# Who makes the last fourteen low halves of the probabilities, and when the first batch's rows are sent

## The reference, cut to what matters

```python
q, k, v = (x @ W for W in (Wq, Wk, Wv))             # 2 x 1024 x 16 x 64
w = softmax(einsum('bihd,bkhd->bhik', q, k) / 8)
x = layernorm(x + einsum('bhij,bjhd->bihd', w, v).reshape(b, s, 1024) @ Wo + bo)
logits = ...                                         # 8 per token, from a small softmax over x @ wqkv.T
top, idx = top_k(logits, 2); scores = softmax(top)
he = silu(x @ w1[e, :352].T) * (x @ w1[e, 352:].T) @ w2[e].T   # e: each of the token's two experts
out = layernorm(x + sum of the two he, weighted by scores)
```

## Time and profile before

| | us |
|---|---|
| median of 3 runs (lowest to highest) | 865.77 (865.43 to 865.95) |
| the profiled execution, its own time | 863.55 |
| span of the profile | 861.8 |
| PE busy | 765.6 (89%) |
| ACT busy | 687.8 (80%) |
| POOL busy | 673.9 (78%) |
| DVE busy | 537.6 (62%) |
| L882, the low halves on POOL | 541.0, 256 of 2.13 |
| L783 and L784, the two exponentials on ACT | 286.3 and 284.9, 256 of each |
| L429, the sends of rows on POOL | 32 of 0.99 |

### The profile page before, as it was taken

The page is one execution under the profiler, slowest core; times in us unless marked ns, Lnnn a source line. Parts: engine busy times, 40 slices in busy tenths (PEclk is TensorE's granted clock), DMA queues, the critical chain, the costliest instruction groups (busy, mean ns, idle before and its releaser), DMA issues. The chain is left out here.

```text
span 861.8 us, 22282 instructions
## 1 busy us (share of the span) xinstructions
PE 765.6 (89%) x9183; PEld 525.2 (61%) x9183; DVE 537.6 (62%) x907; ACT 687.8 (80%) x854; POOL 673.9 (78%) x430
## 2 busy tenths in 40 slices
PE   2889999999999999999999999999988657839991
PEld 0346565666666666666666666666655446729990
DVE  6856667666666676666866667766653167515673
ACT  3899999998989898999999898989889755214452
POOL 5799888888888797888898789999999962554441
PEclk9999999999999999999999999999999987959996
DMA  5603064303031211213040404031200041121212
GB/s 174 150 2 75 5 139 82 78 2 78 8 72 27 53 39 41 54 27 75 5 108 5 112 2 111 14 99 39 48 11 17 11 117 44 36 71 51 79 40 86
DMA packets 43138, 49.30 MB, mean 57 GB/s; under 512 B 6785, under 2 KB 27655, under 8 KB 42912
## 3 DMA queue, kind: packets, MB, share of 16 engines
q1 hardware_dynamic: 39872, 43.31, 20.4%
q0 software_dynamic: 2496, 4.24, 1.5%
q10 hardware_dynamic: 672, 0.33, 0.2%
HBM read 14.28 MB, written 9.25 MB: 27 GB/s over the span
## 5 line engine op out<-in xcount | busy, mean ns | idle before, releaser
L882 POOL TENSOR_TENSOR pl<-p,ph 128x1024 f16<-128x1024 f32 x256 | 541.0, 2130 | 70.2 <-ACT ph L784 69.6
L944 DVE TENSOR_REDUCE mx<-mps 128x1 f32<-128x1024 f32 x249 | 303.8, 1220 | 133.7 <-PE mps L619 131.6
L783 ACT ACTIVATE p<-sps,escale 128x1024 f32<-128x1024 f32 x256 | 286.3, 1118 | 51.2 <-PE sps L599 45.6
L784 ACT ACTIVATE ph<-sps,escale 128x1024 f16<-128x1024 f32 x256 | 284.9, 1113 | 0.0
L694 PE MATMUL pair_bank<-v,ph 128*128 128x65 f16 x2048 | 214.7, 193 | 16.8 <-POOL pl L882 15.2
L694 PEld LDWEIGHTS pair_bank<-v,ph 128*128 128x128 f16 x2048 | 190.4, 96 | 55.7 <-POOL pl L882 25.2
L696 PE MATMUL pair_bank<-v,ph 128*128 128x64 f16 x2048 | 214.4, 195 | 0.0
L698 PE MATMUL pair_bank<-v,pl 128*128 128x65 f16 x2048 | 214.0, 192 | 0.0
L696 PEld LDWEIGHTS pair_bank<-v,ph 128*128 128x128 f16 x2048 | 190.0, 97 | 27.6
L598 PE MATMUL sps<-q_hh,k_hl 128*128 128x512 f16 x512 | 194.1, 379 | 1.8 <-ACT ph L784 1.5
L599 PE MATMUL sps<-q_lm,k_h 65*128 65x512 f16 x512 | 194.7, 380 | 0.0
(11 more groups left out here) (256 smaller groups left out, 966.8 us busy)
## 6 DMA issues: line engine op xcount, KB each, us to landing
q_hh<-hi SPq DMA_DIRECT2D x60, 128.0 KB, 2.3
q_lm<-lo SPq DMA_DIRECT2D x30, 128.0 KB, 2.4
k_h<-hi SPq DMA_DIRECT2D x30, 128.0 KB, 2.5
k_hl<-hi SPq DMA_DIRECT2D x29, 128.0 KB, 2.6
k_hl<-lo SPq DMA_DIRECT2D x29, 128.0 KB, 2.6
sorted<-pad SPq DMA_DIRECT2D x1, 2990.0 KB, 16.8
xb<-sorted SPq DMA_DIRECT2D x46, 65.0 KB, 1.8
v<-in_w1T SPq DMA_DIRECT2D x8, 352.0 KB, 3.5
```

The lines of the kernel that those rows point to most:

```text
L783: nc.scalar.activation(p32[:, n % 4, :], sps[:, n % 2, :], ACT.Exp, bias=EXP_BIAS, scale=escale[:, 0:1])
L784: nc.scalar.activation(ph[:, n % 4, :], sps[:, n % 2, :], ACT.Exp, bias=EXP_BIAS, scale=escale[:, 0:1]).then_inc(s_exp, 1)
L882: nc.gpsimd.tensor_tensor(pl[:, n % 4, :], p32[:, n % 4, :], ph[:, n % 4, :], ALU.subtract).then_inc(s_subp, 1)
L944: nc.vector.tensor_reduce(mx[:, i // TB, i % TB:i % TB + 1], src, AX.X, ALU.max).then_inc(s_mx, 1)
```

## The change

The low halves of steps 242 to 255 are made by DVE instead of GpSimd, with a semaphore of their own, `s_subv`, on which PE's `values` waits from step 242 on. DVE makes that of step n + 2 at the end of its slot n, behind whatever else the slot holds and ahead of its part of the routing. All sixteen sends of batch 0 now stand in the attention loop: four in pair 14 (steps 2, 6, 10, 14) where six stood, and twelve in steps 1 to 12 of pair 15, where GpSimd has no low halves any more beyond step 1. `passed` moves from step 9 of pair 15 to step 0, DVE's first part of `owner` from step 10 to step 3. The loop over the last four sends at the beginning of the second block goes.

```diff
-              ("vector", 13, 11, "where", 0), ("pool", 13, 15, "where", 1), ("pool", 15, 9, "passed", 0),
-              ("vector", 15, 10, "owner", 0), ("pool", 15, 14, "owner", 1))
-SEND_AT = {divmod(PCH * 14 + (8 * n) // 3, PCH): n for n in range(12)}
+              ("vector", 13, 11, "where", 0), ("pool", 13, 15, "where", 1), ("pool", 15, 0, "passed", 0),
+              ("vector", 15, 3, "owner", 0), ("pool", 15, 14, "owner", 1))
+SEND_AT = {(14, 2): 0, (14, 6): 1, (14, 10): 2, (14, 14): 3, **{(15, n - 3): n for n in range(4, 2 * TB)}}
+LAST_LOW = PCH * (PAIRS - 1) + 2
...
+        s_subv = sem("s_subv")
...
-                pe.wait_ge(s_subp, n + 1)
+                if n < LAST_LOW:
+                    pe.wait_ge(s_subp, n + 1)
+                else:
+                    pe.wait_ge(s_subv, n + 1 - LAST_LOW)
...
-                    low_parts(PCH * pp + s)
+                    if PCH * pp + s < LAST_LOW:
+                        low_parts(PCH * pp + s)
...
+            def last_low_parts(n):
+                dve.wait_ge(s_exp, n + 1)
+                nc.vector.tensor_tensor(pl[:, n % 4, :], p32[:, n % 4, :], ph[:, n % 4, :],
+                                        ALU.subtract).then_inc(s_subv, 1)
...
                         take_front(kind, k, job + number)
+                    if LAST_LOW <= n + 2 < PAIRS * PCH:
+                        last_low_parts(n + 2)
                     front_at(nc, dve, "vector", f, pp, s)
...
         @block.gpsimd
         def _(pool):
-            for n in range(len(SEND_AT), 2 * TB):
-                send_row(nc, f, io, 0, n)
             row_ids(nc, f, 1, s_ids)
```

## The result

The changed kernel took 863.67 us (median of 8 runs, 860.18 to 865.43) beside 865.57 (864.87 to 865.95) for the kernel before on the same chip: a ratio of 0.9976, 95% interval 0.9966 to 0.9986. The gain is 1.9 us where 9.3 were forecast. The profiled execution took 863.75 us, with a span of 861.4; the kernel before had 861.8 in its profile. Note the spread: 5.2 us between its runs, 1.1 between those of before.

What follows compares the result with a forecast made beforehand. The prediction took GpSimd's queue to bound the loop's end. With ACT next, the last values would begin at 684.0 instead of 693.3, a gain of 9.3 us: 865.77 - 9.3 = 856.5 us, range 854.4 to 859.6.

Steps and rivals of the forecast that it cites:

- the bound and its removal: Loop's end, 655 to 694 us: GpSimd's queue bounds, busy 36.93 of 39 us; fourteen low halves go to DVE.
- The gain in pair 14: Pair 14 of the loop: two sends fewer on GpSimd gain 1.4 us, at most 2.3.
- The duration of a low half on DVE: Steps 242 to 255: each low half takes DVE 1.22 us, between 1.2 and 1.4.
- The hold at the crossing: Steps 241 to 242: GpSimd's low half holds DVE's first until 654.8; step 245 begins at 658.7, costing 1.4 us.
- ACT as the next bound: Steps 245 to 254 in pair 15: ACT's two exponentials set the pace, 2.02 us a step.
- The tail: Loop's end behind step 254: a chain of jobs sharing one bank; last values begin at 684.0 instead of 693.30.
- Sends in pair 15: Pair 15: twelve sends, 15.2 us from 654.8, done by 670.0, well ahead of the end; cost nothing.
- The mixture was taken to move along unchanged: Behind the loop: first cast at 685.9 instead of 695.19, every later stretch as long as before.
- B: Rival, pair 15: steps stay above 2.02 us, as sends hold low halves or engines miss each other; 858.3 to 859.5; chance 0.09.
- C: Rival, pair 15: DVE's low half of step 242 held through all twelve sends, 15.2 us; 871.7 us; chance 0.04.
- A: Rival, steps 241 to 242: DVE not held, more gained in pair 14; 854.5 to 855.4 us; chance 0.12.
- D: Rival, mixture: loop's gain never arrives, as the mixture waits for something unmoved, such as weights' transfers; 865.8 us; chance 0.02.

Runs made afterwards that it cites:

- The kernel with rests: The changed kernel plus a GpSimd memset of 128x768 behind each of pair 15's twelve sends; 857.40 us, 0.9917 of the kernel before.
- the version without the crossing: The changed kernel, but DVE takes over low halves from step 244, sends move two steps later, each waiting for its step's exponentials; 855.17 us.

## Why the prediction was wrong

*Right:* the bound and its removal (GpSimd 36.93 to 17.20 us). The gain in pair 14: PE's waits for low halves fell from 3.0 to 1.5 us, and about 1.2 us were gained (1.4 forecast). The duration of a low half on DVE, 1.20 to 1.23 us undisturbed, for 1.22. The hold at the crossing, but not all of its price: step 245 began 2.0 us later than it would have with no hold (658.67 + 1.2 - 1.4 = 658.5, against 660.47), for a forecast 1.4, since ACT's issue of the row, 0.63 us, was put at nothing. ACT as the next bound at 2.0 us a step, wherever signals come in time. The tail: from the start of step 254 to the first cast 9.25 us (684.09 to 693.34) for a forecast 9.0.

*Failed:* the step "Sends in pair 15", costed at **nothing**. It counted GpSimd's time for the twelve sends and asked whether that time lay beside other work; it did. What it left out is what close sends can do to the others' signals. In the sum: the forecast put the cast at 685.9, it came at 693.34, 7.4 us later. Of these 1.2 are the offset of this execution, 0.6 the issue at the crossing (660.47 against 658.7 + 1.2), 0.2 the tail, and 5.4 the nine steps from 245 to 254, which took 684.09 - 660.47 = 23.6 us in place of 9 x 2.02 = 18.2. The kernel with rests, in which only this cause is taken away, has its cast at 686.48, 8.7 us before that of the kernel before, and its median is 7.2 below. The mixture was taken to move along unchanged; it did within 1.5 us (cast to end 166.6 before, 168.1 after). Why it took 1.5 us longer stays open, and so the agreement of 1.85 us at the cast with 1.9 in the medians is partly chance: the two profiled spans differ by 0.4.

The prediction sought its evidence in sends beside *DVE's work in the mixture* and found their durations steady. The durations were the wrong column: the cost stood in the other engines' idle time next to those very rows, as 3.17 and 9.11 us of PE waiting for "issue". A chain with 8.5 and 9.1 us in "another core or an unknown queue" and "issue" on a kernel of one core should have been asked about before anything was costed at nothing.

*Rivals.* B foresaw steps above 2.02 us, for the wrong reason: in it each send holds the low half. It is the other way round: up to 1.86 us for a send that starts beside a running low half, while low halves stay at 1.23 (up to 1.34 in the version without the crossing), and no wait in the loops without late signals comes of it; it keeps the sends apart. C (DVE held through the train) didn't occur: the second low half began at 658.36 between sends. A fell with 2.47 us at the crossing. D came close in size by luck (865.8 against 863.67): the gain was not lost in the mixture; the loop never made most of it.

The Trainium skill (SBUF — State Buffer, Who interferes with whom) would have an instruction like DVE's subtraction leave descriptor writing alone, and marks this as inferred. These runs don't decide against it: a send is held if a subtraction is running when it starts (or starts 0.07 us behind it), to 1.86 us at most beside a single one, and one that began earlier keeps its 0.96 us. An indirect send also reads its row numbers (`where_i`) from SBUF; a hold of that read would look the same, and no run tells them apart. For the low half against GpSimd's low half its rule of a full block holds (2.47 and 2.48 us).

**Open.** Why close indirect DMAs delay the signals of other engines: no run separates the issue of the sends from their transfers, or from the recording of the trace. And why they sometimes don't: eight sends in 9 us at the mixture's beginning delayed nothing, while in the changed loop's trace the signal of PE's values due at 662.0 came at 665.2, when only the sends of 660.71 and 662.04 had come close. Shown is that the delay goes, in the loop, when the same sends are spaced out by memsets and nothing else is edited, and that it shrinks in the mixture.

## What to carry to other kernels

An engine set free runs ahead, and a train of its DMAs does not come free of cost because the engine has time for it: ask at which distance they will follow and whether the trace has such a train already, and read what the *other* engines do beside it. Idle time put down to "issue" or "remote" on a kernel of one core, with the producer long finished, is a finding, not noise; if GpSimd's indirect DMAs stand 1.3 us apart there, try spreading them. Here 1.52 us gained 9.5 us in one kernel and 4.0 in another, and 1.78 us left no wait for "remote", but the last must still land before it is needed. And hand over work between DVE and GpSimd where neither has something urgent behind it: two steps later, ACT's wait at the crossing was gone.

## What the runs showed of the hardware that was not expected

- Indirect DMAs of GpSimd with 128 rows, down to 1.27 us apart: signals of PE 1.6 to 3.1 us late behind the scores in the loop, idle stretches of up to 13 us in the mixture. In the mixture 1.38 us apart gave the same total time as 1.27, 1.52 9.5 us less, and at 1.78 the waits for "remote" are gone. Eight such sends at the mixture's beginning delayed nothing.
- A GpSimd indirect DMA that starts while a DVE subtraction with two inputs in SBUF runs ends 0.8 to 0.95 us behind it (1.02 to 1.86 us in place of 0.96). One that started 0.07 us ahead of six in a row took 5.79 us; one that starts 0.2 us or more ahead is not stretched.
- Adding 0.38 us of useless work to each of 48 instructions on an engine (18 us in all) made the kernel 9.5 us faster.
